# Second layer of four experts: weights held and 512 tokens moved, gates spread over partitions through HBM

## What is computed

```python
h = gelu(einsum('bsd,edh->ebsh', x, w1) + b1[:, None, None, :])
y = einsum('ebsh,ehd->ebsd', h, w2) + b2[:, None, None, :]
out = einsum('bse,ebsd->bsd', masked, y)
```

## Time and profile before

| | |
|---|---|
| median of 3 runs | 471.73 us (471.09 to 473.12) |
| span of the profiled execution, first to last instruction | 469.8 us |
| what the median has beyond that span | 1.9 us |
| PE busy / its weight loads | 429.3 us (91%) / 344.1 us (73%) |
| DVE, ACT, POOL busy | 57%, 56%, 31% |
| chain that ended last, share of the span | PE 73%, DVE 12%, ACT 5% |
| second layer's matmuls in that chain (L1018) | 18% |
| recurrence and first projections | up to 101 us |
| the second layer of the last block, then its store | from 453.5 us |

### The profile page before, as it was taken

One profiled execution on the slowest core, in us unless ns is written; L12 is line 12 of the kernel. 1 busy time (PEld: TensorE's weight loads), 2 busy tenths in 40 slices (PEclk: granted clock), 3 DMA queues, 4 the chain that ended last, 5 costly groups with the idle time before them and its releaser, 6 DMA issues.

```text
span 469.8 us, 10623 instructions
## 1 busy us (share of the span) xinstructions
PE 429.3 (91%) x3112; PEld 344.1 (73%) x3112; DVE 269.8 (57%) x954; ACT 263.7 (56%) x740; POOL 146.5 (31%) x309
## 2 busy tenths in 40 slices
PE   6999995449779999999999999999999999999897
PEld 6989994325558767877787787778767877787676
DVE  3888887445523853585277527743763586267424
ACT  2444453236557556664866485568556664866370
POOL 5000000235521542254236215531543254235200
PEclk9999998557979999999999999999999999999999
DMA  8500000031021002100210121012002100210000
GB/s 201 130 0 0 0 0 0 17 71 32 3 57 29 19 0 59 44 17 14 66 38 0 38 51 28 0 46 52 19 0 54 46 0 4 76 22 3 7 11 17
DMA packets 14392, 14.93 MB, mean 32 GB/s; under 512 B 5426, under 2 KB 11412, under 8 KB 14372
## 3 DMA queue, kind: packets, MB, share of 16 engines
q1 hardware_dynamic: 14180, 14.30, 12.1%
q0 software_dynamic: 192, 0.39, 0.3%
HBM read 3.86 MB, written 1.57 MB: 12 GB/s over the span
## 4 chain that ended last, share of the span: by engine, by line
PE 73%; DVE 12%; ACT 5%; issue 5%; SPq 2%; DMA 1%; POOL 1%; DVEq 1%; ACTq 0%; POOLq 0%
PE F L1018 18%; PE T L976 9%; PE A L997 8%; PE F L1034 4%; PE F L1038 4%; PE S L960 4%; PE F L1035 4%; PE S L962 3%; PE F L1014 3%; PE S L965 2%; DVE c L629 2%; DVE ig L627 2%; ACT tc_sb L471 2%; DVE pt_sb L457 1%; PE M L939 1%
## 5 line engine op out<-in xcount | busy, mean ns | idle before, releaser
L406 POOL TENSOR_SCALAR p_sb<-p_sb,rden 128x128 f32<-128x128 f32 (+1 forms) x192 | 79.8, 431 | 135.0 <-DVE rden L710 132.8
L1018 PE MATMUL F<-w_sb,hid 128*128 128x96 f32 x768 | 101.0, 276 | 0.0
L1018 PEld LDWEIGHTS F<-w_sb,hid 128*128 128x128 f32 x768 | 93.4, 192 | 6.0 <-issue 6.0
L518 ACT ACTIVATE p_sb<-S,nmax 128x128 f32<-128x128 f32 (+1 forms) x192 | 78.9, 425 | 17.1 <-DVE nmax L704 17.0
L704 DVE TENSOR_REDUCE nmax<-S 128x2 f32<-128x512 f32 (+1 forms) x80 | 50.7, 634 | 52.7 <-PE S L965 52.3
L457 ACT COPY pt_sb<-T 128x512 f32<-128x512 f32 (+1 forms) x48 | 26.4, 550 | 68.7 <-PE T L976 68.7
L564 ACT ACTIVATE hid<-F,b_sb 128x512 f32<-128x512 f32 x72 | 49.3, 686 | 9.6 <-PE F L1038 9.0
L997 PE MATMUL A<-pt_sb,v_cur 128*32 128x128 f32 x576 | 44.2, 284 | 8.5 <-ACT pt_sb L457 4.5
L976 PE MATMUL T<-id_sb,p_sb 128*128 128x128 f32 x288 | 49.2, 290 | 1.5 <-POOL p_sb L406 1.4
L960 PE MATMUL S<-k_bd,q_st 96*128 96x384 f32 (+2 forms) x96 | 39.3, 416 | 6.5 <-DMA k_bd<-k_cur 6.4
L976 PEld LDWEIGHTS T<-id_sb,p_sb 128*128 128x128 f32 x288 | 30.9, 143 | 16.3 <-issue 13.9
(11 more groups left out here) (140 smaller groups left out, 781.8 us busy)
## 6 DMA issues: line engine op xcount, KB each, us to landing
k_bd<-k_cur SPq DMA_DIRECT2D x96, 32.0 KB, 2.0
q_st<-q_cur SPq DMA_DIRECT2D x28, 96.0 KB, 2.2
k_bd<-k_cur SPq DMA_DIRECT2D x96, 16.0 KB, 1.8
t_st<-t_cm SPq DMA_DIRECT2D x7, 192.0 KB, 2.4
out_y<-y_sb SPq DMA_DIRECT2D x7, 192.0 KB, 1.9
x_pad<-in_x SPq DMA_DIRECT2D x2, 612.0 KB, 8.6
w_sb<-in_w SPq DMA_DIRECT2D x1, 576.0 KB
hid<-in_w SPq DMA_DIRECT2D x1, 576.0 KB, 6.9
```

What stands on the lines that cost most here:

```text
L406: last = nc.gpsimd.tensor_scalar(p, p, rden[:, u % 3, i:i + 1], 1.0, ALU.mult, ALU.mult)
L518: last = nc.scalar.activation(p_sb[:, u % 3, i * nk:(i + 1) * nk], S[u % 2][:, i * nk:(i + 1) * nk], ACT.Exp, bias=nmax[:, u % 3, i:i + 1] ...
L1018: last = mm(dst[:, e * C:(e + 1) * C], hid[:, c, s * TT:(s + 1) * TT], w2_sb[:, c], start=False, stop=(c == NCH - 1), skip_group_check=True)
```

## The change

The second layer is turned round. `w2_sb[:, c]` (128x96) is now the stationary operand and all 512 tokens of `hid[:, c]` move, so a block takes 12 matmuls, and expert e's result is a bank of its own with the 96 channels on partitions and the tokens along it. The bias is a column that DVE adds; the bias matmuls and their setup are gone.

A gate now has to stand on every partition, along the tokens. PE transposes `gw` to 16x128 (`turn_gates`, slot 1), ACT copies it to `gate_t`, SP writes that to HBM, waits for it, and reads it back to all 96 partitions as `gates_cm`, 96x2048 (`spread_gates`, behind `t_st`). DVE's `combine(n, e)` computes (bank + bias) * gate for 96x512 and, for experts 1 to 3, adds it to `y_cm` with a second instruction. The combines of experts 0, 1 and 2 stand in slots 4, 5 and 7 (`COMBINE_AT`), that of expert 3 behind `x2lo`. PE turns `y_cm` back to tokens on partitions with four transposes (`turn_y`, in the first layer's stretch), and DVE's `finish`, behind the first part of `route`, adds `t1p` in one instruction of 128x384. POOL's `keep_t1` and SP's store wait for `finish`.

`FILL` deals the 12 matmuls out as 4, 1, 1, 1, 1, 1 and then none; two of the last three stand before the transposes of the normalized tokens, one behind. Expert 3 uses the bank of expert 1, so its first matmul waits until expert 1 is combined.

```diff
-FILL = [16, 3, 3, 2, 3, 3, 2, 2, 2, 0]
-TAIL = SPB * NCH - sum(FILL)
-TAIL_EARLY = min(TAIL, 9)
+FILL = [4, 1, 1, 1, 1, 1, 0, 0, 0, 0]
+TAIL = NCH - sum(FILL)
+TAIL_EARLY = min(TAIL, 2)
+COMBINE_AT = (4, 5, 7)
...
-        L2 = [F[0], F[2], F[1], F[2]]
+        Y = [F[0], F[1], F[2], F[1]]
+        GT = F[2]
...
+            def spread_gates(n, first=False):
+                wait_alone(sp, gate_copied, n + 1)
+                sp.dma_start(gate_hbm.rearrange("e s t -> s e t"), gate_t[:]).then_inc(gate_out, 16)
+                wait_alone(sp, gate_out, 16 * n + 16)
+                if not first:
+                    wait_alone(sp, gated, E * n)
+                sp.dma_start(gates_cm[:], gate_hbm.rearrange("e s t -> (e s t)").unsqueeze(0).to_broadcast((C, E * BT))
+                             ).then_inc(gate_in, 16)
...
-            for s0, s1 in ((0, SPB - 1), (SPB - 1, SPB)):
-                sp.wait_ge(comb, 16 * (NBLK - 1) + 4 * s1)
-                sp.dma_start(out[NBLK - 1, :, s0:s1], y_sb[:, s0:s1]).then_inc(y_out, 16)
+            spread_gates(NBLK - 1)
+            store_y(NBLK - 1)
...
+            def take_gates(n):
+                act.wait_ge(gate_turned, n + 1)
+                nc.scalar.copy(gate_t[:], GT[0:SPB * E, 0:TT]).then_inc(gate_copied, 1)
...
-                for e in range(E):
-                    if e:
-                        dve.wait_ge(comb, 16 * n + 4 * s + e)
-                    V.scalar_tensor_tensor(y_sb[:, s], L2[s][:, e * C:(e + 1) * C], gw[:, s, e:e + 1],
-                                           t1p[:, s] if e == 0 else y_sb[:, s], ALU.mult, ALU.add).then_inc(comb, 1)
+                dst = y_part[:, e % 2] if e else y_cm[:]
+                V.scalar_tensor_tensor(dst, Y[e][0:C, :], b2_sb[:, e:e + 1], gates_cm[:, e], ALU.add, ALU.mult
+                                       ).then_inc(gated, 1)
+                if e:
+                    dve.wait_ge(gated, E * n + e + 1)
+                    if e > 1:
+                        dve.wait_ge(summed, (E - 1) * n + e - 1)
+                    V.tensor_tensor(y_cm[:], y_cm[:], dst, ALU.add).then_inc(summed, 1)
+            def finish(n, first):
+                dve.wait_ge(y_turned, n + 1)
+                dve.wait_ge(t1p_done, n + 1)
+                if not first:
+                    dve.wait_ge(y_out, 16 * n)
+                V.tensor_tensor(y_sb[:], T[:, 0:SPB * C].rearrange("p (s c) -> p s c", c=C), t1p[:], ALU.add
+                                ).then_inc(y_done, 1)
...
-                    last = mm(dst[:, e * C:(e + 1) * C], hid[:, c, s * TT:(s + 1) * TT], w2_sb[:, c],
-                              start=False, stop=(c == NCH - 1), skip_group_check=True)
+                    last = mm(dst[0:C, :], w2_sb[:, c], hid[:, c, :], start=(c % CPE == 0), stop=(c % CPE == CPE - 1))
...
-            for s in range(SPB):
-                expert_out(NBLK - 1, [(s, c) for c in range(NCH)])
+            expert_out(NBLK - 1, range(2 * CPE))
+            turn_gates(NBLK - 1)
+            expert_out(NBLK - 1, range(2 * CPE, NCH))
+            turn_y(NBLK - 1)
```

More of the change, by code:

```diff
@@ L267, in out_parts @@
         def out_parts(slot):
-            return [divmod(i, NCH) for i in range(sum(FILL[:slot]), sum(FILL[:slot + 1]))]
+            return range(sum(FILL[:slot]), sum(FILL[:slot + 1]))
         def wait_alone(eng, semaphore, value):
@@ L353, in body @@
                     stage(n + 2)
+                if not first:
+                    spread_gates(n - 1, first=not store)
             sp.wait_ge(zeroed, 5)
@@ L547, in body @@
                         take_x1(n + 1)
+                    if j == 1 and not first:
+                        take_gates(n - 1)
                 heads_out(n, SPB - 1, first)
@@ L798, in body @@
                         x1_rest(n + 1)
-                    if not first and j:
-                        for s, c in out_parts(j - 1):
-                            if c == NCH - 1:
-                                combine(n - 1, s, second)
+                    if not first and j in COMBINE_AT:
+                        combine(n - 1, COMBINE_AT.index(j), second)
                     if not last:
@@ L821, in body @@
                 if not first:
-                    for s in range(sum(FILL[:-1]) // NCH, SPB):
-                        combine(n - 1, s, second)
+                    for e in range(len(COMBINE_AT), E):
+                        combine(n - 1, e, second)
                 route(n, 0)
+                if not first:
+                    finish(n - 1, second)
                 if not last:
@@ L842, in _ @@
             route(NBLK - 1, 2)
-            for s in range(SPB):
-                combine(NBLK - 1, s, False)
+            for e in range(E):
+                combine(NBLK - 1, e, False)
+            finish(NBLK - 1, False)
         @block.tensor
@@ L1030, in expert_hidden @@
                     elif not first:
-                        pe.wait_ge(comb, 16 * n - 16 + 4 * (c + 1))
+                        pe.wait_ge(gated, E * n - E + 1 + max(e for e in range(E) if Y[e] is L1[c]))
                     cs = slice(c * 128, (c + 1) * 128)
@@ L1040, in body @@
             def body(n, first=False, last=False):
-                tail = [divmod(i, NCH) for i in range(SPB * NCH - TAIL, SPB * NCH)]
+                tail = range(NCH - TAIL, NCH)
                 for j in range(NU):
@@ L1050, in body @@
                         start = [] if first else out_parts(0)
-                        expert_out(n - 1, start[:NCH])
+                        expert_out(n - 1, start[:CPE])
                         scores(n, 2)
-                        expert_out(n - 1, start[NCH:])
+                        expert_out(n - 1, start[CPE:])
+                    if j == 1 and not first:
+                        turn_gates(n - 1)
                     probs_t(n, j, first)
@@ L1099, in body @@
                 expert_hidden(n, range(3, 6), first)
+                if not first:
+                    turn_y(n - 1)
                 wait_alone(pe, route_copied, n + 1)
```

85 lines of the change are left out of this document (51 added, 34 removed).

## The result

The changed kernel takes 500.28 us (median of 4 runs, 498.29 to 501.82), the kernel before beside it 471.41 (470.94 to 473.12): 1.0612 times as long, 95% interval 1.0565 to 1.0658. It is slower, as forecast, by 29 us in place of 15, and lies 0.3 us above the upper end of the range. The profiled execution has a span of 500.0 us.

What follows compares the result with a forecast made beforehand. PE, held in slots 6 to 9 by the four-engine round, was taken to bound the kernel. 469.8 us plus 8.4 for the bodies and 7.0 for the end gave 485.2, with 1.9 from span to median 487; range 473 to 500.

Steps and rivals of the forecast that it cites:

- the term of the body: Loop body: late transposes of units 7 and 9 plus `turn_y` make each body 1.3 us longer.
- The end: Last block: 7 us more, 4.3 from the longer chain and 2.7 from expert 3's matmuls at half clock.
- the third rival: Gates read from HBM takes 7 to 9 us, expert 0 waits 2 to 4 us per body: 504 us, chance 0.10.
- What bounds the kernel: PE sets the pace; in slots 6 to 9 the round through four engines does, so work before DVE's reciprocals moves PE.
- The long matmul: PE's second layer: 512 moving columns at two clocks each cost 0.427 us and a little, 0.88 us per two-record matmul.
- PE's saving and where it lies: Per block 1.6 us less PE work; 1.5 us of saving lies in slots 6 to 8, where PE waits anyway.
- DVE's walk: Slots 4 to 9: experts 1 and 2 cost 1.3 us each, transposes of unit 7 0.8 late, of unit 9 0.9.
- The gates: Read of 768 KB from HBM takes 4.0 us, landing when DVE reaches expert 0; 1 us of DVE idle covers further delay.
- PE's work decides: Rival: DVE's additions fit its gaps, each of 7 bodies saves 1.6 us, the end costs 4.3: 465 us, chance 0.14.
- The sum: Whole execution: 469.8 plus 8.4 for bodies and 7.0 for the end gives 485.2, with 1.9 more 487 us.

Runs made afterwards that it cites:

- the long wait filled: Changed kernel with five extra one-pass 512-column matmuls, result unused, ahead of the transposes in slot 7 of every block but the first: 486.95 us.
- The late sums: Changed kernel with the DVE sums of experts 1 and 2 moved from slots 5 and 7 to slots 8 and 9: 475.36 us.
- the filled waits: Changed kernel with extra unused matmuls before the transposes: four in each of slots 6, 7 and 8, 492.16 us; five in slot 7 alone, 486.95 us.
- the spread version: Kernel with the late sums, nine long matmuls of the slots dealt 2, 1, 1, 1, 1, 1, 1, 1 over slots 0 to 7: 481.69 us.
- the one with a matmul in slot 8: Kernel with the late sums, one long matmul moved from slot 0 to slot 8: 473.23 us.
- the old form of the end without HBM: Kernel with the late sums and one matmul in slot 8, its last block's second layer in the form before the change: 466.39 us.

## Why the prediction was right, and where it failed

**The step that failed** is the term of the body, "a body is **1.3 us longer**". It priced PE's waits and nothing that follows from them. The waits are as priced: with the long wait filled, a body takes 45.4 for 44.2, 1.2 us. Over the seven bodies the spans of that run add up to 450.9 - 132.7 = 318.2 us, against 310.5 before: 7.7 us, where 8.4 was forecast. What was left out is the clock: 23.3 - 7.7 = 15.6 us in all. Body by body against the run with the wait filled that is 5.3 us in the first (52.0 for 46.7, with 13.7 us at the lower level in its slots), 2.3 in each of the four middle ones (6.8 us at that level), 0.8 in the sixth and 0.3 in the seventh. I had the means for it. The end's sum has half a clock in it, from the earlier trace rows, and the third rival says that PE's waits "could cost it the clock as well". But I took the pause of 2.5 us in the earlier trace rows for the kind of pause it takes, and did not ask what waits of 0.8 and 0.9 us on top of the 0.4 to 0.5 that were there add up to, in slots from which the matmuls had just been taken. Had the body's term had a second case, "and the clock falls for 6.8 us", 3.4 us of PE's work in it would have been the upper bound, 7 x 3.4 = 24 on 487, and the range would have reached past 500.

**What bounds the kernel.** Right. The round DVE, POOL, PE sets the time in slots 6 to 9, and what stands in front of a reciprocal moves PE. The late sums show it most plainly.

**The long matmul.** Twelve records take 5.31 us in a row with the tail of the last one, 0.43 each, as forecast from columns at two clocks. As the filling of a slot, a pair takes 0.95 us to the next start, not 0.88; with five slots that is, as an estimate, 0.35 us more per body.

**PE's saving and where it lies.** Half right. That the saving of slots 6 to 8 turns into waits was right. Its other side I had not priced: matmuls in such a wait can keep PE's clock, as the filled waits show. That the six short ones had done so is argued, not shown. In slot 0 the four long matmuls cover waits as well, as the spread version and the one with a matmul in slot 8 show.

**DVE's walk.** Right to 0.1 us: 1.38 for an expert (1.3), transposes of unit 7 0.85 late (0.8). That expert 2 in slot 7 delays unit 9 by about as much is not what came: PE does not wait for POOL's scaling in slot 9, and the two instructions cost some 0.4 us by themselves. `finish` and POOL's work behind it are hidden, as said.

The Trainium skill ("SBUF — State Buffer", SBUF: two separate sides) has a DVE instruction with two SBUF inputs and a GpSimd one that reads SBUF exclude each other for a whole instruction, for which the prediction had up to 0.9 us per body aside. In the changed kernel nothing of it shows. The sum of expert 1 starts 0.77 us after the instruction ahead of it, with POOL idle; that of expert 2 0.87 us after (267.86 to 268.73), but POOL's scaling had ended at 268.49, and that of expert 3 also 0.87 (280.40 to 281.27), with POOL idle. In the kernel with the late sums the trace agrees with the rule, on POOL's side: a scaling that starts 0.03 us behind the sum of expert 1 takes 1.03 us, where none in the changed kernel takes over 0.49.

```profile
256.75 0.70 DVE L811 TENSOR_TENSOR y_cm<-y_cm,y_part 96x512 f32<-96x512 f32 x1
256.78 1.03 POOL L432 TENSOR_SCALAR p_sb<-p_sb,rden 128x256 f32<-128x256 f32 x1
```

**The gates.** The read takes 4.9 us, not 4.0. DVE waits 0.7 to 0.8 us for them in a loop body, in time that it had free; the cover that I put at 1 us beyond the landing was 0.2 in the kernel with the late sums, the only one in which it was measured. The Trainium skill ("DMA: Bandwidth & Descriptors", Anatomy of one DMA) fits 2.0 us plus the bytes at 436 GB/s to DMAs that GpSimd issues; for 768 KB that would be, as an estimate, 3.8 us. This read is issued by SP, and the measured 4.9 decides.

**The end.** 7.2 us for 7.0, a match by luck, since two errors cancel. From the first matmul to the start of expert 3's there are 14.2 us (476.38 to 490.55), for 12.9 forecast, by the slower read and what stands around it; and those matmuls lie at the lower clock only until 493.7, so that six records take 4.38 us and not 5.3. A bank of its own for expert 3 takes 3.1 us off the kernel with the late sums, and the old form of the end without HBM 7.7 (34.9 to 27.2).

**The rivals.** That PE's work decides (465 us) was wrong for the change as made, and right for the mechanism: with nothing ahead of the reciprocals the bodies are 0.5 to 0.7 us shorter than before. Its condition, that experts 1 and 2 hold DVE for less than 0.6 us each, was too narrow; they may hold it for 1.4, at another place. The rival nearest to the measured time, the late gates with 504 us, is near it by luck: DVE waited 0.7 us for the gates, not 2 to 4 beyond its cover. But its words that PE's waits could cost the clock as well name what happened, from another wait.

**The sum.** 469.8 + 7.7 + 7.2 + 15.6 of clock, less 0.3 in front, is 500.0. The forecast's own sum has two slips that weigh nothing: the last body is 1.3 - 0.6 = 0.7, not 0.6, and the end 472.0 + 1.9 = 473.9, not 474.1.

**What stays open.** Why the same waits are followed by a fall of the clock in some bodies and not in others, and why the lower level lasts 13.7 us in the first body of the changed kernel and 6.8 in the middle ones, after waits that are alike (1.58 and 0.86, 1.60 and 0.86). The bodies with 0.22, 0.86 and 0.48 us kept their clock in all slots, those with 1.60 and 0.86 mostly lost it, and of those with 0.67 and 0.86 one did, the first.

## What to carry to other kernels

A wait of TensorE has two prices: its own length, and what it does to the clock of the work behind it. In an engine that is 98% busy the second can be the larger, here 2.3 us beside 1.2, so every forecast of new waits on PE needs a case in which the clock falls, with PE's work in that stretch as its bound. Before moving DVE work into a software-pipelined round, look for the small instruction there on which the others hang (here a reciprocal of 0.15 us) and put the long ones behind it, not ahead. And matmuls that seem to be load may be cover: take them out of a slot only after asking what ran behind them.

## What the runs showed of the hardware

- The granted clock went to 0.50 after PE waits of 1.60 and 0.86 us, one soon behind the other: for 6.8 us in the middle bodies, for 13.7 in the first. Five added one-pass matmuls of 512 columns in the longer wait, whose result nobody uses, kept it at 1.00 and saved 13.3 us in all.
- With the same waits in each body the fall came in some and not in others of one execution (bodies of 45.0 and 47.7 us).
- A pair of 512-column float32 records costs 0.86 us in a row of them and 0.95 us between other work.
- A GpSimd scaling that ran beside a DVE sum of two SBUF tiles took 1.03 us; in the changed kernel, where none ran so, it took at most 0.49.
- Reading 8 KB of HBM out to 96 partitions, 768 KB in all, takes 4.9 us to landing, though a store of 192 KB took 1.9.
